# Graph attention, 8192 nodes, 4 heads, one core: s and d by a thin matmul from x kept turned on the chip, the projection later, V's tables made out of the banks

## The reference: what is computed

```
xt = einsum('ni,hio->hno', x, W)
src = einsum('hnf,hf->hn', xt, a[:, :64])
dst = einsum('hnf,hf->hn', xt, a[:, 64:])
e = leaky_relu(src[:, :, None] + dst[:, None, :], 0.2)
e = where(adj > 0, e, -inf)
h = einsum('hij,hjf->hif', softmax(e, axis=2), xt)
out = layernorm(x + h.transpose(1, 0, 2).reshape(n, 256))
```

## Time and profile before

| | us |
|---|---|
| median of 3 runs | 2275.49 (2274.74 to 2275.79) |
| the profiled execution | 2278.14 |
| its span, first to last instruction | 2275.9 |
| TensorE matmul busy | 2080.7 (91%) |
| VectorE busy | 2098.8 (92%) |
| ScalarE busy | 2011.4 (88%) |
| GpSimd busy | 126.9 (6%) |

### The profile page before, as it was taken

The page is one execution under the profiler, slowest core; times in us unless marked ns, Lnnn a source line. Parts: engine busy times, 40 slices in busy tenths (PEclk is TensorE's granted clock), DMA queues, the critical chain, the costliest instruction groups (busy, mean ns, idle before and its releaser), DMA issues.

```text
span 2275.9 us, 79541 instructions
## 1 busy us (share of the span) xinstructions
PE 2080.7 (91%) x34180; PEld 2051.7 (90%) x34180; DVE 2098.8 (92%) x2334; ACT 2011.4 (88%) x2045; POOL 126.9 (6%) x88
## 2 busy tenths in 40 slices
PE   7702799999999999999999999999999999999996
PEld 6601799999999999999999999999999999999996
DVE  4587999999999999999999999999999999988785
ACT  2235699899999999999999999999999999999995
POOL 0063000001000000001000100001000100000000
PEclk9955999999999999999999999999999999999998
DMA  8746967776776667666766667666766667523310
GB/s 293 244 165 254 350 207 242 249 236 198 233 239 208 210 213 246 220 212 206 242 221 211 202 212 244 220 215 208 245 213 214 209 210 252 182 77 83 100 50 20
DMA packets 236578, 469.69 MB, mean 206 GB/s; under 512 B 14656, under 2 KB 23104, under 8 KB 236224
## 3 DMA queue, kind: packets, MB, share of 16 engines
q1 hardware_dynamic: 231600, 447.53, 60.2%
q0 software_dynamic: 4352, 16.78, 2.0%
q10 hardware_dynamic: 272, 0.13, 0.0%
HBM read 438.83 MB, written 25.56 MB: 204 GB/s over the span
## 4 chain that ended last, share of the span: by engine, by line
PE 49%; DVE 16%; ACT 15%; issue 8%; DVEq 1%; POOL 0%; ACTq 0%; POOLq 0%
PE acc L760 46%; ACT big L394 14%; DVE big L566 5%; DVE big L573 5%; PE tp L725 2%; DVE nat L488 1%; ACT big L412 1%; DVE big L558 1%; DVE stats L619 1%; DVE AT L502 1%; DVE big L580 1%; DVE nat L486 1%; ACT big L406 0%; DVE big L588 0%; DVE big L605 0%
## 5 line engine op out<-in xcount | busy, mean ns | idle before, releaser
L394 ACT ACTIVATE big<-big,d_all 128x1024 int8<-128x1024 f32 x1792 | 1896.0, 1141 | 92.0 <-PE acc L760 89.4
L760 PE MATMUL acc<-big 128*128 128x130 f16 x32768 | 1917.5, 220 | 26.4 <-DVE big L580 18.1
L760 PEld LDWEIGHTS acc<-big 128*128 128x128 fp8e5 x32768 | 1892.6, 98 | 37.5 <-issue 33.4
L566 DVE SCALAR_TENSOR_TENSOR big<-big,AT 128x1024 uint32<-128x1024 uint32 x512 | 624.1, 1219 | 74.1 <-ACT big L394 66.3
L573 DVE SCALAR_TENSOR_TENSOR big<-AT,big 128x1024 uint32<-128x1024 uint32 x512 | 623.4, 1218 | 4.5
L725 PE MATMUL tp<-ident,nat 128*128 128x128 f32 x1024 | 157.1, 276 | 130.4 <-DVE nat L486 112.8
L725 PEld LDWEIGHTS tp<-ident,nat 128*128 128x128 f32 x1024 | 109.8, 142 | 136.4 <-issue 130.1
L558 DVE TENSOR_SCALAR big<-big,d_all 128x1024 uint8<-128x1024 f32 x256 | 191.8, 749 | 0.0
L486 DVE TENSOR_SCALAR nat<-raw 128x2048 fp8e4<-128x2048 int32 x128 | 176.3, 1380 | 10.2 <-DMA raw<-in_adj_dram 9.8
L488 DVE TENSOR_SCALAR nat<-raw 128x2048 uint8<-128x2048 int32 x128 | 177.4, 1386 | 0.0
L502 DVE SCALAR_TENSOR_TENSOR AT<-AT,tp 128x512 uint32<-128x512 uint32 x224 | 153.3, 684 | 1.5
(11 more groups left out here) (48 smaller groups left out, 370.3 us busy)
## 6 DMA issues: line engine op xcount, KB each, us to landing
raw<-in_adj_dram SPq DMA_DIRECT2D x256, 1024.0 KB, 5.5
big<-v_parts SPq DMA_DIRECT2D x512, 260.0 KB, 3.7
v_parts<-big SPq DMA_DIRECT2D x16, 1040.0 KB, 4.2
big<-s_rows SPq DMA_DIRECT2D x32, 512.0 KB, 5.5
AT<-in_x_dram SPq DMA_DIRECT2D x16, 512.0 KB, 4.1
big<-in_x_dram POOLq DMA_DIRECT2D x8, 1024.0 KB, 7.9
out_dram<-big POOLq DMA_DIRECT2D x8, 1024.0 KB, 8.5
big<-in_L_gnn_W_dram SPq DMA_DIRECT2D x2, 128.0 KB, 2.5
```

The lines of the kernel that those rows point to most:

```text
L394: return nc.scalar.activation(sgn[:, g % NB, b, :], srow[:, h % 2, :], ACT.Sign, bias=dflat[:, r:r + 1], scale=-1.0)
L566: nc.vector.scalar_tensor_tensor(out=word(sgn, g % NB), in0=word(sgn, g % NB), scalar=EDGE[plane], in1=edges(g), op0=ALU.bitwise_and, op1= ...
L760: return nc.tensor.matmul(acc[:, k, o:o + 2 * VO], m[:, g % NB, b, t * P:(t + 1) * P], Vr[:, v:v + 2 * VO], start=opens, stop=False, skip_ ...
```

## The change

- `xT` holds all 16 groups (in the space of `xt`), `xg` has four buffers in place of two. The turned x goes to banks 0 to 3 in turn.
- `thin(g)`: s and d alone come from `xT` by 8 matmuls with the 8 last columns of `Wx`, all into bank 4. VectorE reads the maximum, s and d from that bank once, after group 15.
- `project(g)` comes after it, without the 8 columns, into two halves of banks 0 to 3. `table(g)` multiplies straight out of the banks by e1 and by e2, both on VectorE. `xt` and the copies into it are gone. GpSimd only copies the columns of e.
- Six mask units (`EARLY`) are made in stage A, ten beside the tables (`made_with`).
- The loops over groups are written out. ScalarE makes the signs of the first four groups of pass 0 beside the tables 9, 11, 13 and 15.
- SP loads 11 of the 16 V blocks of pass 0 beside the tables, as soon as the `xT` under them has been used. The waits for the last stores move: SP waits before it loads the last V blocks, GpSimd before it loads residual x, ScalarE before its first use of `u`.
- The regions of `big` are laid out anew.

More of the change, by code:

```diff
@@ L104, in gat_residual_norm @@
         a_in = sem("a_in")
-        x_in = [sem("x_in0"), sem("x_in1")]
+        x_in = [sem(f"x_in{n}") for n in range(NX)]
         ident_set = sem("ident_set")
@@ L110, in gat_residual_norm @@
         xT_done = sem("xT_done")
-        xt_done = sem("xt_done")
-        xt_kept = sem("xt_kept")
+        thin_done = sem("thin_done")
+        s_kept = sem("s_kept")
+        proj_done = sem("proj_done")
         mx_done = sem("mx_done")
@@ L243, in load, with load_x @@
                 sp.dma_start(raw[:, u % 4], adj_v[2 * c + u % 2, u // 2]).then_inc(raw_in[u % 4], 16)
-            with sp.Fori(0, NG // 4) as i:
-                for n in range(4):
-                    sp.wait_ge(xTp_done, 4 * i + n + 1)
-                    sp.dma_start(xg[n % 2], x_v[4 * i + n]).then_inc(x_in[n % 2], 16)
-                    sp.wait_ge(conv_done, 4 * i + n + 1)
-                    sp.dma_start(raw[:, n], adj_v[n % 2, 2 * i + n // 2]).then_inc(raw_in[n], 16)
-            for k in range(NG, NG + 4):
-                load(0, k)
+            def load_x(g):
+                sp.dma_start(xg[g % NX], x_v[g]).then_inc(x_in[g % NX], 16)
             def load_rows(c, h):
@@ L308, in _ @@
             nc.gpsimd.partition_all_reduce(M[:, :], mx[:, :], P, RMAX).then_inc(M_done, 1)
-            with pool.Fori(0, NG // 2) as i:
-                for n in range(2):
-                    g = 2 * i + n
-                    pool.wait_ge(scaled, 2)
-                    pool.wait_ge(lo_done, g + 1)
-                    nc.gpsimd.tensor_tensor(out=U2[n][:, :, :, 0:O], in0=xt_of(g), in1=e_of(e2, g),
-                                            op=ALU.mult).then_inc(U2_done, 1)
-                    nc.gpsimd.tensor_copy(U2[n][:, :, :, O], e_row(e2, g)).then_inc(U2_done, 1)
+            pool.wait_ge(scaled, 2)
[4 more added lines that the diff above has]
+                nc.gpsimd.tensor_copy(U2[g % 2][:, :, :, O], e_row(e2, g)).then_inc(ecol_done, 1)
             def load_res(c, n):
@@ L503, in keep @@
                                                    op0=ALU.bitwise_and, op1=ALU.bitwise_or).then_inc(at_done, 1)
-            for g in range(NG):
-                convert(g, g, 0)
-                leave(g)
-                if g:
-                    keep(g - 1, g - 1, 0, fresh=True)
-            dve.wait_ge(xt_kept, NG + 1)
-            nc.vector.tensor_reduce(mx[:, :], d_all[:, :, :].rearrange("p r h -> p h r"), AX.X, ALU.max).then_inc(mx_done, 1)
-            keep(NG - 1, NG - 1, 0, fresh=True)
+            for k in range(EARLY):
[8 more added lines that the diff above has]
+            dve.wait_ge(s_kept, 2)
             dve.wait_ge(M_done, 1)
@@ L537, in lows @@
                                                op0=ALU.mult, op1=ALU.add).then_inc(lo_done, 1)
-            table1(0, 0)
-            with dve.Fori(0, HALF - 1) as i:
-                table1(2 * i + 1, 1)
-                lows(2 * i, 0)
-                dve.wait_ge(lo_done, 2 * i + 3)
-                table1(2 * i + 2, 0)
-                lows(2 * i + 1, 1)
-                dve.wait_ge(lo_done, 2 * i + 4)
-            table1(NG - 1, 1)
-            lows(NG - 2, 0)
-            lows(NG - 1, 1)
-            dve.wait_ge(lo_done, NG + 2)
-            for n in range(2):
-                dve.wait_ge(v_out[n], 16 * (HALF + 1))
+            for g in range(NG):
[8 more added lines that the diff above has]
+            dve.wait_ge(row_in[0], 16)
             def compares(n, g, h):
```

96 lines of the change are left out of this document (21 added, 75 removed).

## The result

| | before | after |
|---|---|---|
| median, us (4 runs each, same chip) | 2275.11 (2272.82 to 2275.79) | 2377.96 (2370.86 to 2385.07) |
| the profiled execution, us | 2278.14 | 2385.07 |
| its span, us | 2275.9 | 2383.5 |
| maximum of d starts | 102.57 | 90.13 |
| last low part of V ends | 204.67 | 193.60 |

The ratio is 1.0448 [1.0433, 1.0463]: 103 us slower, where 44 us faster was forecast. The lead-in did get shorter, by 14.6 us up to the third group of sums. The other side is the loop over passes, which the diff doesn't touch: 24 passes cost 5.2 us more each.

The account below looks back on a forecast made before the run. TensorE was taken to set stage A, a shared limit stage B, and the steady part to stay unchanged. -42.6 (stage A) + 3.8 (stage B) - 6 (hand-over) = -44.8 off the median 2275.49 gave 2231 us, range 2222 to 2274.

Parts of the forecast that it names:

- The failed step: Steady part after the first 300 us: claimed unchanged by the change, so nothing was added for it.
- Stage A: Lead-in up to the maximum, x turned and projected: thin matmuls at full clock bring the maximum to 60.0, 42.6 us earlier.
- the first rival: Half clock all through stage A: maximum at 96.7, 36.7 us later than forecast, total 2268; chance 0.30.
- The half-clock sum: Stage A at half clock: thin steps of 3.44 us from 13.2 on, turns and mask turns, maximum at 96.7.
- The argument for the full clock: Stage A: full clock from 18.2 us on, as stretches before a fall idled 1.8 us or more and this has none.
- The rival on the slower side: Stage A: weight loads bind at half clock, 0.34 us per thin instruction, maximum at 128, total 2299; chance 0.10.
- Stage B: Making V's tables after the maximum, set by VectorE: 105.9 us against 102.1 before, 3.8 more.
- GpSimd's late start: Start of stage B: GpSimd's first copy still comes 12.7 us after the maximum; without this, 3.3 us shorter.
- bound below: Lower bound for stage B, without GpSimd's delay: 99.5 us.
- Hand-over and pass 0: From the last table into the first masked sums: earlier signs and row loads gain 6 us (range 2 to 10).
- The sum of the lead-in: All three lead-in terms together, -42.6 + 3.8 - 6: 44.8 us saved.
- the half-clock rival: Half clock through stage A, the same as the first rival: total 2268; chance 0.30.

Follow-up runs that it names:

- wide: a_pad32 with each thin matmul streaming up to 128 columns in place of 8: 2226.46 us, ratio 0.9785.
- early11: a_pad32 with eleven mask units made in stage A in place of six, and the loads in that order: 2250.13 us, ratio 0.9888.
- a_pad32: The changed kernel with 32 semaphore increments more at the start of TensorE's stream: 2261.56 us, ratio 0.9933.
- nosigns: a_pad32 without ScalarE's early signs of four groups beside the tables; they are made after the last table: 2261.94 us, ratio 0.9944.
- a_pad8: The changed kernel with 8 semaphore increments more at the start of TensorE's stream: 2384.48 us.
- a_pad16: The changed kernel with 16 semaphore increments more at the start of TensorE's stream: 2258.45 us, ratio 0.9929.

## Why the prediction was wrong

- **The failed step** is "The change leaves that part as it is, so every microsecond comes from the first 300." The diff leaves the loop's text as it is, but not its place in TensorE's program, and the place decided 116 of the 2378 us (2377.96 - 2261.56). Each pass took 68.22 us in place of 63.03, by a stall on an instruction fetch and the half clock behind it. The prediction put this term at nothing, no rival had it, and the time lies 104 us above the range.
- **Stage A**: the mechanism of the first rival, chance 0.30, was right. Predicted 60.0 at full clock and 96.7 at half; it was 90.1. The half-clock sum was 6.6 too long: the first thin instructions start at 11.93 and not at 13.2; a thin step is 3.28 from its start to that of the turns behind it (11.93 to 15.21) and not 3.44, 2.6 us over sixteen steps; and some 5 us ran at full clock from 64.6, where 32 thin instructions took 4.5 in place of 6.8 and the turns between them 1.07 in place of 1.95. The prices per instruction were both right: 0.215 at half clock, and 0.12 at full (1.95/16 with 128 columns in `wide`, 1.85/16 with 8 in early11's stretch), against 0.11.
- The argument for the full clock, that each fall in the earlier trace rows had idle time before it and the new stage has none, fell: TensorE had no gap and stayed at half but for one stretch. The Trainium skill's warning, "TensorE: Matmul & The Clock Gate", Part 4, pointed the right way, but the turns alone don't hold the clock down: `wide` has the same turns and ran them in 1.04 us.
- **The rival on the slower side**, loads that bind at 0.34 us, did not occur.
- **Stage B**: 103.5 us, predicted 105.9 (before 102.1). The price of reading the banks was right (1.22 us, predicted 1.23). GpSimd's late start, kept in the sum for 3.3 us, was gone: its first copy came 4.1 us behind the maximum. The stores took something back: 46.3 us of ScalarE's waits, of which 2.6 reached VectorE. The "bound below" of 99.5 was not reached.
- **Hand-over and pass 0**: the sums start 6.3 us behind the last low part, predicted 7. The raw block of unit 20 comes 23.5 behind it (217.11 - 193.60), predicted 20; third sums 28.7, predicted 26; before 32.2. So 3.5 us of gain where 6 were forecast.
- **The sum of the lead-in**: -12.4 + 1.4 - 3.5 = -14.5; read directly it is -14.6 (222.28 - 236.86). With the loop in a good place the whole kernel shows it: a_pad32, 12.2 us faster than its own before (2261.56 against 2273.72), where the half-clock rival said 2268. With the clock held too, `wide` is at 2226.5, close to the 2231 of the forecast, in part by luck. Its maximum was 4.1 us earlier than forecast (55.93 against 60.0) and its stage B 5.1 shorter (100.8 against 105.9), while the way to the third sums was 2.7 longer (28.7 against 26) and a pass of the loop 0.19 longer than before's (63.22 against 63.03), 4.6 us in 24 passes. The terms were near, and what the forecast missed is what the change did to the program's layout and to the clock.

## What to carry to other kernels

Code added anywhere ahead of a long loop moves the loop in its instruction blocks. When a loop that wasn't touched gets slower by the same amount in each pass, look for "issue" waits at one fixed instruction and count the instruction queue's packets; some idle instructions in front tell whether it is that (here 8 left it and 16 cured it). Matmuls that stream few columns for each weight load (8 here) can leave TensorE at half clock even when it is never idle, and streaming more columns can then be faster. An order of loads has a price of its own: look at what is queued ahead of the last needed block, and not only at what is computed beside it.

## What was not expected of the hardware

- One block of instructions more in each pass cost 5 us of 63: a gap of 3.65 us in the mean (80.3/22) and the half clock behind it.
- In stage A the clock rose by itself while nothing in the pattern changed: at 64.6 us in after, 53.6 in a_pad32, at 11.9 and 39.7 in `nosigns`, and at 54.8 in `early11`, where it held for four groups and came again near 75. The timeline of TensorE in early11:

```profile
53.13 1.92 PE L731 MATMUL acc<-ident,AT 128*128 128x128 f32 x8
54.84 1.91 PE L740 MATMUL acc<-big 128*128 128x8 f32 x16
```

  Its steps after 57 are 1.85 us for 16 thin instructions, from 57.94, 60.99 and 64.04 on. No run tells what raises the clock. The maximum of after, a_pad8, a_pad16, a_pad32 and `nosigns`, which have the same stage A, lies between 84.1 and 90.2 for this.
- The column of the granted clock can't be read before its first change. After shows 1.00 from 20 to 30 us with 49 matmuls; `nosigns` shows 0.50 in the same stretch with 50. The pace (eight turns in 1.95 us) is half in both.
- A semaphore increment in TensorE's stream takes 0.15 us: the maximum comes 14.05 us later with 205 of them than with 109 (125.91 and 111.86).
- GpSimd's 12.7 us between the maximum and its first product are not there when its first work behind the reduction is a plain copy. The Trainium skill, "GPSIMD Engine Reference" (wrapper-ucode dispatch), gives about 6 us for the first use of a kernel that must be loaded. The wait here was longer, 11.62 us of "issue", so the page's load could be a part of it; no run put a product back, and the cause is not shown.
